# Edge attention on a graph: tile chains by matrix products instead of scans, with the adds moved into the loop's last bodies

## The reference

```python
q, k, v = (layer_norm(x @ W[h]) for W in (Wq, Wk, Wv))        # per node and head
ke, ve = (layer_norm(x_edge @ W[h]) for W in (Wke, Wve))      # per edge and head
rel_k = layer_norm(concat([ke, k[:, src]], -1) @ relk_W + relk_b)
qk = sum(q[:, dst] * rel_k, -1) / 4
lse = log(segment_sum(exp(qk - segment_max(qk)[dst]))) + segment_max(qk)
rel_v = layer_norm(concat([ve, v[:, src]], -1) @ relv_W + relv_b)
agg = segment_sum((qk - lse[dst]) * rel_v, dst)
z = layer_norm(relu(agg @ z_W + z_b))
out = layer_norm(x + z)
```

## Time and profile before

| | |
|---|---|
| median of 3 runs | 2994.78 us (2994.47 to 2997.76) |
| the profiled execution's own time | 2993.24 us |
| its span, first to last instruction | 2991.5 us |
| mean granted TensorE clock over it | 0.977 |
| end of the last gather of the loop | 2725.8 us |
| tail begins (POOL's fill, L1687) | 2758.6 us |
| end of the segment scans | 2856 us |
| first final turn | 2889.6 us |

### The profile page before, as it was taken

The page is one execution under the profiler, slowest core; times in us unless marked ns, Lnnn a source line. Parts: engine busy times, 40 slices in busy tenths (PEclk is TensorE's granted clock), DMA queues, the critical chain, the costliest instruction groups (busy, mean ns, idle before and its releaser), DMA issues. The chain is left out here.

```text
span 2991.5 us, 74825 instructions
## 1 busy us (share of the span) xinstructions
PE 2805.4 (94%) x18870; PEld 2486.7 (83%) x18870; DVE 2848.9 (95%) x3072; ACT 2304.7 (77%) x5301; POOL 2396.4 (80%) x2622
## 2 busy tenths in 40 slices
PE   4669999999999999999999999999999999998945
PEld 3349999999999999999999999999999999996633
DVE  6879999999999999999999999999999999998948
ACT  2448888888888888888888888888888888886527
POOL 6768888888888888888888888888888888885773
PEclk8989999999999999999999999999999999999978
DMA  4568888888888888888888888888888888887742
GB/s 89 163 177 242 258 255 257 253 256 252 255 253 257 254 254 253 255 254 255 253 255 253 255 254 254 256 253 251 257 255 253 256 252 254 254 264 215 196 112 56
DMA packets 661200, 703.01 MB, mean 235 GB/s; under 512 B 98801, under 2 KB 555238, under 8 KB 660749
## 3 DMA queue, kind: packets, MB, share of 16 engines
q1 hardware_dynamic: 568897, 491.48, 54.4%
q0 software_dynamic: 84896, 208.11, 25.5%
q10 hardware_dynamic: 7340, 2.66, 0.5%
HBM read 470.00 MB, written 231.15 MB: 234 GB/s over the span
## 5 line engine op out<-in xcount | busy, mean ns | idle before, releaser
L1446 POOL DMA_INDIRECT e_rows<-node_table,e_gcol x1564 | 1911.9, 1222 | 420.2 <-issue 416.1
L1239 PE MATMUL banks<-w_edge,e_eat 128*128 128x240 f32 x6256 | 1397.0, 366 | 0.5 <-ACT e_ysq L1368 0.5
L1239 PEld LDWEIGHTS banks<-w_edge,e_eat 128*128 128x128 f32 x6256 | 1180.6, 190 | 84.5 <-issue 0.7
L1218 PE MATMUL banks<-e_h,e_oh 128*128 128x248 f32 x3128 | 782.9, 373 | 2.9 <-DVE e_h L1552 2.8
L1547 DVE TENSOR_REDUCE e_zs<-e_z 128x96 f32<-128x1440 f32 x391 | 642.7, 1644 | 0.2
L1218 PEld LDWEIGHTS banks<-e_h,e_oh 128*128 128x128 f32 x3128 | 563.5, 190 | 44.9 <-DVE e_h L1552 4.3
L1331 ACT ACTIVATE e_agg<-banks 128x496 f32<-128x496 f32 x782 | 458.0, 586 | 109.9 <-PE banks L1218 103.9
L1535 DVE TENSOR_TENSOR e_p<-banks,e_yr 128x960 f32<-128x960 f32 x391 | 452.5, 1157 | 27.6 <-PE banks L1239 13.7
L1552 DVE TENSOR_TENSOR e_h<-e_p,e_zw 128x960 f32<-128x960 f32 x391 | 449.5, 1150 | 1.2 <-POOL e_zw L1459 1.2
L1346 ACT ACTIVATE e_eat<-banks 128x512 f32<-128x512 f32 x391 | 233.4, 597 | 281.5 <-PE banks L1252 281.5
L1516 DVE TENSOR_TENSOR e_p<-e_p,e_rows 128x960 f32<-128x960 f32 x391 | 449.6, 1150 | 0.0
(11 more groups left out here) (414 smaller groups left out, 2607.2 us busy)
## 6 DMA issues: line engine op xcount, KB each, us to landing
tile_sums<-e_agg SPq DMA_DIRECT2D x391, 496.0 KB
e_q<-q_by_rank SPq DMA_DIRECT2D x1564, 90.0 KB
e_ea<-in_edge_attr SPq DMA_DIRECT2D x390, 256.0 KB
e_rows<-node_table,e_gcol POOLq DMA_INDIRECT x1564
edge_lse<-t_lse_sb SPq DMA_DIRECT2D x14, 448.0 KB, 3.5
edge_qk<-e_qkt SPq DMA_DIRECT2D x130, 48.0 KB
node_table<-n_tb SPq DMA_DIRECT2D x24, 240.0 KB, 2.6
n_x<-in_x SPq DMA_DIRECT2D x24, 128.0 KB, 2.3
```

The source lines that it names most:

```text
L1218: last = nc.tensor.matmul(sums_bank(x, loop, half)[:, (j % 2) * AW:(j % 2 + 1) * AW], oh[:, x % OR, j, :], hh[:, x % HR, j, :, :].rearrang ...
L1239: last = nc.tensor.matmul(out_ps[:, j // 2, (j % 2) * 2 * HC:(j % 2 + 1) * 2 * HC], eat[:, x % 4, j * P:(j + 1) * P], t["w_edge"][:, at:at ...
L1446: g.indirect_dma_start(out=rows[:, k, j, :], out_offset=None, in_=table, in_offset=bass.IndirectOffsetOnAxis(ap=gcol[:, kb, at:at + 1].bit ...
```

## The change

**Matrices instead of scans.** For set k, POOL makes a 128x128 matrix by comparing the chain number of each tile as a row (`seg_row`, the numbers broadcast to all partitions) with that of each partition's tile (`seg_col`): 1 where both tiles carry the same node. A second matrix compares with the number of the last tile of the set before (`last_col`, -1 except in the last partition), so that the running sum at that tile is carried on. PE forms `same.T @ firsts[k] + last_same.T @ firsts[k-1]` (`chain_sum`), ACT copies it over `firsts[k]` (`chain_copy`, one per set), and POOL adds the set (`chain_add`). The table of numbers is made and stored in `start` (one DVE operation, one store and one load more), `last_col` by two DVE operations at the start of `edges`.

**Where it stands.** POOL makes the matrices of two sets at the end of each of bodies 391 to 396 and one at 397 (25 comparisons: 3, then 4 in each of five bodies, then 2), and adds set c-393 in bodies 393 to 399, sets 7 to 11 behind the loop, set 12 in the tail. PE's products are in bodies 392 to 400 and behind them. SP broadcasts the numbers in body 385 and loads two sets of first rows per body in 385 to 389, one in 390. DVE's six scans, PE's transposes both ways and ACT's 15 copies go. In the tail the logits' part 3 waits for nothing more, part 4 also for the last product, part 5 for the 7th maximum instead of the adds.

```diff
-CHAIN_AT = GROUPS + 3
+CHAIN_AT = GROUPS + 1
...
+def chain_mats(t, k):
+    at = PARTS[3][1] * SUB + 2 * P * k
+    return t["x"][:, at:at + P], t["x"][:, at + P:at + 2 * P]
+
+def chain_sum(nc, t, k, bank):
+    same, last_same = chain_mats(t, k)
+    out = bank[:, (k % 2) * 2 * P:(k % 2) * 2 * P + AW]
+    done = nc.tensor.matmul(out, same, t["firsts"][:, k, :], start=True, stop=(k == 0))
+    if k:
+        done = nc.tensor.matmul(out, last_same, t["firsts"][:, k - 1, :], start=False, stop=True)
+    return done
+
+def chain_copy(sc_, t, k, bank):
+    return sc_.activation(t["firsts"][:, k, :], bank[:, (k % 2) * 2 * P:(k % 2) * 2 * P + AW], mybir.ActivationFunctionType.Copy)
+
+def chain_add(nc, t, k, last_sum):
+    return nc.gpsimd.indirect_dma_start(out=t["sums_d"], out_offset=bass.IndirectOffsetOnAxis(ap=t["carry_idx"][:, k:k + 1].bitcast(mybir.dt.uint32), axis=0),
+                                        in_=t["firsts"][:, k, :], in_offset=None, bounds_check=last_sum, oob_is_err=True, compute_op=ALU_ADD)
...
@@ SP, edges @@
-                kk = c - FIRSTS_AT
-                if not loop and (0 <= kk < KT - 2 or c == (KT - 1) * SET_G + STORE_LAG + 1):
...
+                kk = 2 * (c - FIRSTS_AT)
+                if not loop and kk == 0:
+                    sp.dma_start(seg_row[:].rearrange("p k e -> p (k e)"), t["chain_d"].partition_broadcast(P)).then_inc(s_more, 16)
...
+                if not loop and 0 <= kk < KT - 2:
+                    for i_ in range(kk, min(kk + 2, KT - 2)):
+                        load_firsts(i_)
...
                 if not loop and c == ROWS_AT:
                     sp.wait_ge(s_qx, GROUPS)
                     sp.wait_ge(s_pt, GROUPS)
-                    sp.dma_start(chain_views(t)[2], t["chain_d"].partition_broadcast(P)).then_inc(s_more, 16)
@@ PE, edges @@
+            def chain_set(k):
+                pe.wait_ge(s_cl, k + 1)
...
+                if k:
+                    pe.wait_ge(s_cbc, k)
+                chain_sum(nc, t, k, agg_ps).then_inc(s_cs, 1)
@@ POOL, edges @@
+            def make_mats(k):
+                same, last_same = chain_mats(t, k)
+                if k == 0:
+                    pool.wait_ge(s_tr, GROUPS)
+                    pool.wait_ge(s_more, 16)
+                if k == 7:
+                    pool.wait_ge(s_u, GROUPS)
+                ins = g.tensor_scalar(out=same, in0=seg_row[:, k, :], scalar1=seg_col[:, k:k + 1], scalar2=None, op0=ALU.is_equal)
+                if k:
+                    ins = g.tensor_scalar(out=last_same, in0=seg_row[:, k, :], scalar1=last_col[:, k - 1:k], scalar2=None, op0=ALU.is_equal)
+                ins.then_inc(s_cl, 1)
+
+            def add_set(k):
+                pool.wait_ge(s_cbc, k + 1)
+                pool.reg_add(last_sum, sums_less_2, 1)
+                chain_add(nc, t, k, last_sum).then_inc(s_add, 16)
...
                 gathers(c - 3, i, loop, 2)
+                k = c - GROUPS
+                if not loop and k >= 0:
+                    for k_ in range(2 * k, min(2 * k + 2, KT)):
+                        make_mats(k_)
+                    if k >= 2:
+                        add_set(k - 2)
             every(pool, body, GROUPS + 9)
+            for k in range(GROUPS + 9 - GROUPS - 2, KT - 1):
+                add_set(k)
@@ DVE, edges @@
             every(dve, body, GROUPS + 9)
-            dve.wait_ge(s_more, 16)
-            dve.wait_ge(s_cc, 4)
-            for half in range(2):
-                chain_scan(v, t, 0, half).then_inc(s_cs, 1)
...
@@ POOL, tail @@
-            for k in range(KT):
-                pool.wait_ge(s_cbc, k // 2 + 1)
-                g.indirect_dma_start(out=t["sums_d"], out_offset=bass.IndirectOffsetOnAxis(ap=t["carry_idx"][:, k:k + 1].bitcast(u32), axis=0),
...
+            pool.wait_ge(s_cbc, KT)
+            chain_add(nc, t, KT - 1, last_sum).then_inc(s_add, 16)
             pool.wait_ge(s_add, 16 * KT)
@@ SP, tail @@
-                if k == 3:
-                    sp.wait_ge(s_cb, 7)
                 if k == 4:
                     sp.wait_ge(s_m, 4)
+                    sp.wait_ge(s_cs, KT)
                 if k == 5:
-                    sp.wait_ge(s_add, 16 * KT)
+                    sp.wait_ge(s_m, 7)
                     sp.wait_ge(s_low, 16)
@@ DVE, tail @@
-                if k == 0:
-                    dve.wait_ge(s_cc, 7)
-                    dve.wait_ge(s_cs, 4)
-                    for half in range(2):
-                        chain_scan(v, t, 2, half).then_inc(s_cs, 1)
```

More of the change, by code:

```diff
@@ L148, in chain_back @@
-def chain_back(nc, t, tiles, bank):
-    _, st_t, _ = chain_views(t)
-    for j, tile in enumerate(tiles):
-        for half in range(2):
-            w = min(P, AW - half * P)
-            at = (2 * j + half) * P
-            last = nc.tensor.transpose(bank[:, at:at + w], st_t[0:w, half * HALF + tile * P:half * HALF + (tile + 1) * P], t["ident"][0:w, 0:w])
-    return last
-def chain_scan(v, t, part, half):
-    xt_t, st_t, more = chain_views(t)
-    w = min(P, AW - half * P)
-    lo, hi = CHAIN_PARTS[part][0] * P, CHAIN_PARTS[part][1] * P
-    at = half * HALF
-    return v.tensor_tensor_scan(out=st_t[0:w, at + lo:at + hi], data0=more[0:w, lo:hi], data1=xt_t[0:w, at + lo:at + hi],
-                                initial=st_t[0:w, at + lo - 1:at + lo] if lo else 0.0, op0=ALU_MULT, op1=ALU_ADD)
@@ L637, in _ @@
             v.tensor_copy(out=rank_o[:], in_=key_f[:, 0, :]).then_inc(s_ro, 1)
+            v.scalar_tensor_tensor(out=tq[:, 0, :], in0=key_f[:, 0, :], scalar=2.0, in1=linked, op0=ALU.mult, op1=ALU.add).then_inc(s_tq, 1)
             link(v.tensor_scalar(out=base[:], in0=loc[:, 1, :], scalar1=car_ps[:, 1:2], scalar2=None, op0=ALU.max))
@@ L1309, in body @@
                     project(x, i, 2 * HC, u_ps, s_u)
-                if not loop and 0 <= c - CHAIN_AT < 4:
+                if not loop and c >= CHAIN_AT:
                     chain_set(c - CHAIN_AT)
             every(pe, body, GROUPS + 10)
-            for kk in range(4, len(CHAIN_SETS)):
-                chain_set(kk)
-            for kk in range(4):
-                pe.wait_ge(s_cs, 2)
-                pe.wait_ge(s_cc, len(CHAIN_SETS))
-                if kk >= 2:
-                    pe.wait_ge(s_cbc, kk - 1)
-                chain_back(nc, t, (2 * kk, 2 * kk + 1), banks[:, 6 + kk % 2, :]).then_inc(s_cb, 1)
+            for k in range(GROUPS + 10 - CHAIN_AT, KT - 1):
+                chain_set(k)
         @block.scalar
@@ L1413, in body @@
                     nc.scalar.activation(zw[:, x % WR, :, :, 0], zln[:, :, 1:2 * H:2], ACT.Exp, scale=-0.5).then_inc(s_zw, 1)
-                if not loop and 0 <= c - CHAIN_AT < 4:
+                if not loop and c >= CHAIN_AT:
                     copy_set(c - CHAIN_AT)
             every(act, body, GROUPS + 10)
-            for kk in range(4, len(CHAIN_SETS)):
-                copy_set(kk)
-            for kk in range(4):
-                act.wait_ge(s_cb, kk + 1)
-                chain_copy(nc.scalar, t, (2 * kk, 2 * kk + 1), banks[:, 6 + kk % 2, :]).then_inc(s_cbc, 1)
+            for k in range(GROUPS + 10 - CHAIN_AT, KT - 1):
+                copy_set(k)
         @block.gpsimd
@@ L1501, in _ @@
             link(v.tensor_copy(out=p_f, in_=p_i[:, 1:3]))
+            link(v.scalar_tensor_tensor(out=last_col[:], in0=seg_col[:], scalar=1.0, in1=ident[:, P - 1:P].to_broadcast([P, KT]), op0=ALU.add, op1=ALU.mult))
+            link(v.tensor_scalar(out=last_col[:], in0=last_col[:], scalar1=-1.0, scalar2=None, op0=ALU.add))
             link(v.tensor_copy(out=same_c[:], in_=c_i))
```

120 lines of the change are left out of this document (42 added, 78 removed).

## The result

The changed kernel takes 3014.34 us in the median of 4 runs (3013.22 to 3016.52) against 2994.62 of the kernel before; the ratio is 1.0064, 95% interval 1.0052 to 1.0076. The forecast was 2989.3, range to 3003.5: the time lies above the range, on the side of rival B. The profiled span grew from 2991.5 to 3011.4 us, by 19.9.

The account below looks back on a forecast made before the run. PE (94%) and DVE (95%) are busy over the span, but loop end and tail price the change, with POOL ending last in the tail. Lse gathers −6.1 us and clock +0.6 give −5.5: median 2989.3 us, range 2979.5 to 3003.5.

Parts of the forecast that it names:

- rival B: Slower through POOL's comparisons, held or 0.9 us each: loop end grows 14.3 us, to 3003.5, deciding from 0.55; chance 0.18.
- step 5: DVE in the tail: the last chain scans and the wait for ACT's copy go, −2.6 us.
- step 6: POOL's tail: one add instead of 13, sum gathers near 2780; lse stores then bind, lse gathers at 2877.1, gain 6.1 us.
- Steps 1 to 3: Bodies 391 to 399: POOL's comparisons and adds delay DVE's row scaling; group 390 is scaled 14.5 us later, at 2757.3.
- Step 4: Behind the loop: POOL's adds of sets 6 to 11 end at 2768.3, the tail starts 10.5 us late, at 2769.2.
- Step 7: Final turns: beta adds end at 2890, 6 us of delay absorbed by turns 2 to 5's waits; clock adds 0.6 us.
- The +0.6 put down for the clock: A thinner end of the loop may lower the granted clock: 0.6 us, a tenth of the gain, as a guess.
- Rival C: Final turns: the 6 us gained at the lse gathers are lost to later beta adds, giving 2994.8 us; chance 0.17.

Follow-up runs that it names:

- e7: Changed kernel with POOL's twelve adds all behind the loop's bodies, comparisons left in place: 3007.41 us, ratio 1.0041.
- e12: Kernel before, with SP's wait for the adds ahead of part 5 replaced by the wait for the 7th maximum: 2997.32 us, ratio 1.0002.
- e5: Changed kernel without the 7th-maximum wait ahead of part 5, set 12's product behind the second piece, comparisons on DVE: 2991.06 us, ratio 0.9983.
- e3: Changed kernel without the 7th-maximum wait ahead of part 5 and with set 12's product behind the second piece: 2998.62 us, ratio 1.0009.
- e4: Changed kernel with the 25 comparisons on DVE instead of POOL, at the end of the same bodies: 3010.77 us, ratio 1.0055.
- e1: Changed kernel without SP's wait for the 7th maximum ahead of part 5: 3004.35 us, ratio 1.0029.
- e2: Changed kernel with PE's product for set 12 behind the second piece's products, ACT's copy behind its exps: 3003.79 us, ratio 1.0028.
- e9: Changed kernel with set 12's load ahead of the load of the logits' part 2: 3004.45 us, ratio 1.0027.
- e10: Version e5 with the adds of sets 7 to 11 behind the fill in the tail and set 12's load ahead of part 2: 2996.99 us, ratio 1.0004.

## Why the prediction was wrong, step by step

The forecast was 5.5 us less, measured are 19.7 more. The step that failed worst is step 5, with the wait in step 6 beside it; the drain's price comes third.

- **Steps 1 to 3, the drain: mechanism right, size low.** The comparisons stand behind the wait and ahead of L1460, as said, and the steps between DVE's rows were 8.05, 6.35, 5.34, 5.30, 4.37, 3.01 against 8.06, 5.57, 4.5, 4.5, 3.84, 3.18 forecast. The failed term is the comparison's price, "I take 0.33, nearest to the smaller select": it was 0.60, near the larger select of 0.67 in the earlier trace rows. The add, taken at 1.4, kept POOL 1.15. That body 393 came out at 8.05 against 8.06 is luck: its L1468, put down as held for 2.46, took 0.26; the two gathers took 3.1 instead of 2.34, and the comparisons 2.4 instead of 1.32.
- **Step 4, the tail's start: +13.6 (1.0 of it older than the drain), not +10.5, and for another reason.** The tail's start, taken as "0.86 later" than the end of POOL's adds of sets 6 to 11, doesn't stand behind these: e7 shows that they aren't waited for. The last three sets' products and copies behind the loop set it, one set per 1.64 us up to 2771.5. These were a term put at nothing ("The two matmuls per set I cost at nothing", and the copy with them); they had no cover there. SP was at the stage's end at 2770.8, so these cost 1.2 us at the most.
- **Step 5, −2.6: the step that failed worst.** I removed DVE's scans and their wait but did not ask what had taken their place at the head of PE's and ACT's tail, and what that waits for. The product of set 12 waited for a load behind 1.3 MB: +6.3 instead of −2.6.
- **Step 6: "SP's early waits for the adds and back-transposes go too, covered by the scans."** The wait for the adds did not just go, it was replaced by a later one, and I did not name what was queued behind it: the lse stores, for which ACT has two buffers. Cost 9.0 us. With the three misses (3.1 in step 4, 8.9 in step 5, 9.0 here) the forecast lse gathers at 2877.1 become 2898.1; measured 2898.74. That it closes to 0.6 is partly luck, since traces of one kernel differ by more.
- **Step 6, "the lse stores are late next": right**, and by far more than said: 11.55 us. The sum gathers, forecast near 2780, start at 2792.55: set 12's add was issued at 2781.91, not 2771, and POOL waited 9.1 us for the landing.
- **Step 7** forecast beta adds at 2890 and turns that absorb them; e12 bears that out. With all three mended (e5) the median is 2991.06, close to the 2989.3 of the forecast, but by another path and so partly by luck: the tail starts 5.0 later and not 10.5, and the lse gathers (2876.23, forecast 2877.1) stand behind the sum gathers and not behind the stores. With the comparisons left on POOL, as forecast, and the tail mended (e3) it is 2998.62, no gain. The +0.6 put down for the clock is small beside the 3.0 that the turns lose behind the second; how much of these is the clock is not shown.
- **Rival B** had the side and the threshold (0.55) but not the amount: at 0.60 by its own formula −5.5 + 25 x 0.27 = +1.3 us. The sign that it gave, comparisons over 0.55, came true. **Rival C** named beta adds, which set the first turn here and in e5, but the second turn waits for its lse gathers again, so the lead is not lost there. What the Trainium skill says in "GPSIMD Engine Reference", "Engine selection", that elementwise work belongs on VectorE, fits e4: 0.27 us against 0.60, though its one-input case, about line rate, does not fit POOL's 0.60. On descriptor generation the rows stay against the inference in the Trainium skill's "SBUF — State Buffer", "Who interferes with whom": in the changed kernel the gathers at 2720.38 and 2722.47, beside DVE's L1563 and L1527, took 1.8 us, those at 2717.25 and 2718.67 1.1 and 1.0.

## What to carry to other kernels

When a wait in an in-order queue is exchanged, list what is issued behind it and how many buffers its producers have: one semaphore on SP cost 10 us here and nothing measurable in a kernel whose slack hid it. When work leaves an engine, look at what now stands first on the engines that start the next stage, and which queue its data comes through. Price a missing operation by the dearer of two like rows unless something tells them apart. For an engine that looks idle, find where its idle time stands in program order. And before two traces are compared at the end, compare them ahead of the change: here they were 1 to 3 us apart already.

## What the runs showed of the hardware that was not expected

A load of 27 KB issued right behind 1.3 MB on the same queue was usable 10.2 us after its issue, and 3.6 with the order turned. POOL waited 5.2 to 19.5 us behind its last add into DRAM for the adds to land. In e1, e2, e3, e9 and the changed kernel the last add starts 3.8 to 12.0 us behind DVE's entry into the tail, and yet the wait for the landing ends 20.1 to 20.6 us behind that entry in all five: when the last add is issued does not decide it there. That the bulk loads beside them do is a guess; for it speaks the kernel before without its wait for part 5 (10.93 us against 6.34), against it e10, which loads part 3 as early as e5 does and whose adds land 14 us later. DVE's product with two SBUF inputs grew too when comparisons of POOL ran beside it, from 1.15 to 1.38, 1.62 and 1.58 us (once, at 2754.67, it stayed at 1.19); in e4, with the comparisons off POOL and the adds still on it, none of the 391 took over 1.19. The holding goes both ways.
